# Sums over the first attention's products: one strided reduction, or halving adds in place

## The reference, cut to what matters

```python
pQ = elu(Q); pK = elu(K)                    # Q, K, V: [b, s, H, HD]
Q1, Q2 = split(pQ, 2, axis=-1)
K1, K2 = split(pK, 2, axis=-1)
kv1 = einsum('bshe,bshd->bsed', K1, V) * SCALE
kv2 = einsum('bshe,bshd->bsed', K2, V) * SCALE
w1 = einsum('bshe,bsed->bshd', Q1, kv1)
w2 = einsum('bshe,bsed->bshd', Q2, kv2)
attn = w1 - lmb * w2
```

## Time and profile before

| what | us |
|---|---|
| median of the two runs | 4460.06 |
| span of the profiled execution | 4458.2 |
| DVE busy over the span | 2525.6 (57%) |
| POOL busy over the span | 1256.7 (28%) |
| PE busy over the span | 3281.8 (74%) |
| L818, sum of 13 heads, 56 times | 324.6 |
| L815, sum of 3 heads, 56 times | 81.1 |
| L207 on DVE, product of 13 heads, 56 times | 253.8 |

### The profile page before, as it was taken

How to read it: one execution, slowest core, us unless ns; L and a number is a source line. 1 busy time by engine, 2 the same in 40 slices (tenths; PEclk the granted TensorE clock), 3 DMA queues, 4 the chain that set the end, 5 groups by cost and what they waited for, 6 DMA issues and landing times. The chain is left out here.

```text
span 4458.2 us, 53612 instructions
## 1 busy us (share of the span) xinstructions
PE 3281.8 (74%) x17032; PEld 1909.6 (43%) x17033; DVE 2525.6 (57%) x4655; ACT 1616.7 (36%) x3717; POOL 1256.7 (28%) x873
## 2 busy tenths in 40 slices
PE   6667859775977687587759775976774999999910
PEld 5433623452354235333623452453331666666600
DVE  6764857386658656673857486566749111111156
ACT  2435245433634352444236333624440222222222
POOL 6400910271055008201810460064000111111156
PEclk9889979887988798798879887987885999999955
DMA  1130040004000400310040004002212111111156
GB/s 31 21 52 21 1 71 3 21 0 73 2 20 11 63 21 1 48 25 21 1 72 2 20 1 73 2 20 36 28 45 90 47 45 45 45 45 45 43 182 199
DMA packets 172478, 177.41 MB, mean 40 GB/s; under 512 B 31952, under 2 KB 159696, under 8 KB 172240
## 3 DMA queue, kind: packets, MB, share of 16 engines
q1 hardware_dynamic: 159568, 139.78, 14.6%
q0 software_dynamic: 12672, 34.62, 2.6%
HBM read 106.32 MB, written 67.24 MB: 39 GB/s over the span
## 5 line engine op out<-in xcount | busy, mean ns | idle before, releaser
L434 POOL TENSOR_TENSOR work<-QK,VS 128x2048 f32<-128x2048 f32 x128 | 520.1, 4086 | 1734.7 <-DVE QK L764 1734.2
L925 DVE TENSOR_REDUCE NM<-MX 128x1 f32<-128x128 f32 (+7 forms) x1024 | 735.3, 753 | 448.8 <-PE MX L1162 438.5
L652 ACT ACTIVATE PR<-SP_ 128x512 f32<-128x512 f32 (+3 forms) x1536 | 694.0, 489 | 459.8 <-PE SP_ L1196 312.9
L1160 PE MATMUL MX<-KST,work 96*128 96x512 bf16 (+3 forms) x1536 | 444.8, 354 | 270.9 <-DMA work<-scratch_qd 211.5
L1193 PE MATMUL SP_<-work,KST 99*128 99x512 bf16 (+3 forms) x1536 | 469.6, 333 | 69.6 <-ACT PR L652 32.3
L1554 DVE TENSOR_TENSOR AG<-UB,SL 128x512 f32<-128x512 f32 x136 | 94.1, 692 | 500.3 <-PE UB L1584 500.3
L1160 PEld LDWEIGHTS MX<-KST,work 96*128 96x128 bf16 x1536 | 127.3, 103 | 534.8 <-DVE NM L925 225.5
L1209 PE MATMUL OA<-PR,V 128*32 128x512 f32 (+3 forms) x3072 | 327.3, 498 | 3.3 <-ACT PR L652 3.3
L818 DVE TENSOR_REDUCE AT<-work 128x208 f32<-128x3328 f32 x56 | 324.6, 5797 | 0.0
L1070 PE MATMUL OB<-work,ident 128*128 128x256 f32 x1024 | 258.9, 416 | 74.9 <-POOL work L434 74.9
L1531 ACT ACTIVATE SL<-GB 128x512 f32<-128x512 f32 x136 | 81.3, 598 | 602.6 <-PE GB L1584 602.6
(11 more groups left out here) (242 smaller groups left out, 5252.7 us busy)
## 6 DMA issues: line engine op xcount, KB each, us to landing
work<-scratch_qd SPq DMA_DIRECT2D x96, 256.0 KB, 9.4
scratch_y<-Y SPq DMA_DIRECT2D x136, 128.0 KB, 1.7
scratch_qd<-work SPq DMA_DIRECT2D x48, 256.0 KB, 7.7
X<-in_L_attn_x SPq DMA_DIRECT2D x8, 1024.0 KB, 5.7
scratch_x<-X SPq DMA_DIRECT2D x8, 1024.0 KB, 16.2
scratch_h<-A SPq DMA_DIRECT2D x8, 1024.0 KB, 4.6
scratch_flat<-AT SPq DMA_DIRECT2D x8, 1024.0 KB, 6.2
XH<-scratch_x SPq DMA_DIRECT2D x16, 512.0 KB, 4.3
```

The costliest lines, as they stand in the source:

```text
L434: sg["prod1"].by(pool.tensor_tensor(P1[t % 2][:, i * hh * D:(i + 1) * hh * D].rearrange("p (h e d) -> p h e d", h=hh, e=HD), QK[:, t % 3, ...
L652: sg["exp"].by(act.activation(PR[:, n % 8, q0:512], SP_[:, n % 2, q0:512], ACT.Exp))
L925: sg["mx"].by(dve.tensor_reduce(NM[:, qt, h:h + 1], src, AX.X, ALU.max, negate=True))
L1160: m = pe.matmul(out, lhsT, KST[0:MROW, g, k0:k1], start=True, stop=not last)
```

## The change: what it does

Each of the three sums over e becomes four `tensor_tensor` adds, which work in the buffer of the products. Rows 8 to 15 of every head are added onto rows 0 to 7; then 4 rows onto 4; then 2 onto 2; and the last add, 1 onto 1, writes into `AT`. After each of the first three DVE waits for it to be done (signal `fold`), since the next one reads what it wrote. The signals to the other engines are as before and hang on the last add. For 13 heads the adds have 1664, 832, 416 and 208 elements in each partition, for 3 heads 384, 192, 96 and 48, and for the 4 heads of the last tile 512, 256, 128 and 64.

```diff
+                def fold_rows(x, out, done):
+
+                    rows = x.rearrange("p (h e d) -> p h e d", e=HD, d=HD)
+                    n = HD // 2
+                    while n > 1:
+                        sg["fold"].by(dve.tensor_tensor(rows[:, :, 0:n], rows[:, :, 0:n], rows[:, :, n:2 * n], ALU.add))
+                        sg["fold"].settle(dve)
+                        n //= 2
+                    done.by(dve.tensor_tensor(out.rearrange("p (h d) -> p h d", d=HD), rows[:, :, 0], rows[:, :, 1], ALU.add))
+
                 def attended_last():
...
-                    sg["attn"].by(dve.tensor_reduce(AT[:, u, 0:n * HD].rearrange("p (h d) -> p h d", d=HD),
-                                                    P2[:, 0:n * D].rearrange("p (h e d) -> p h d e", e=HD, d=HD),
-                                                    AX.X, ALU.add))
+                    fold_rows(P2[:, 0:n * D], AT[:, u, 0:n * HD], sg["attn"])
...
                     dve.wait_ge(sg["share2"].sem, u + 1)
                     c0 = (H - POOL_HEADS) * HD
-                    sg["attn"].by(dve.tensor_reduce(AT[:, u, c0:D].rearrange("p (h d) -> p h d", d=HD),
-                                                    PP[:, u % 2].rearrange("p (h e d) -> p h d e", e=HD, d=HD), AX.X, ALU.add))
+                    fold_rows(PP[:, u % 2], AT[:, u, c0:D], sg["attn"])
                     sg["prod2"].settle(dve)
-                    sg["attn"].by(dve.tensor_reduce(AT[:, u, 0:c0].rearrange("p (h d) -> p h d", d=HD),
-                                                    P2[:, 0:(H - POOL_HEADS) * D].rearrange("p (h e d) -> p h d e", e=HD, d=HD),
-                                                    AX.X, ALU.add))
+                    fold_rows(P2[:, 0:(H - POOL_HEADS) * D], AT[:, u, 0:c0], sg["attn"])
```

## The result

The changed kernel takes 4747.8 us (median of two, 4747.0 to 4748.6) against 4460.06: a ratio of 1.065, 95% interval 1.063 to 1.067. That is 288 us slower. The forecast was 4752, with a range of 4682 to 4830. The profiled execution has a span of 4746.7 us, beside the 4458.2 of the earlier trace rows.

A forecast was written before the change was run, and what follows sets the result against it. The prediction took a port shared by DVE's two-SBUF-input instructions and POOL as the bound, 12.79 us a step. Lengthened steps add 36.5 us a batch, x 8 = 292, giving 4750 profiled, 4752 us as a median; range 4682 to 4830.

The forecast's parts named there:

- the port: Something two-SBUF-input DVE instructions and POOL instructions both read through, held for the whole instruction; 12.79 us a step before.
- The exclusion: A DVE instruction with two SBUF inputs and a POOL one cannot run together; a 3328-element product holds POOL off 3.49 us.
- The turns: In each step DVE's product and small adds alternate with POOL's instructions, big adds follow undisturbed; a step becomes 18.2 us.
- The price alone: Adds on DVE without POOL: 3.89 us for 13 heads, 1.39 for 3, against 7.15 for both reductions.
- The sum: Losses of steps 2 to 8 and the last tile added up: 36.5 us a batch, x 8 = 292.
- Rival 1: Adds do not collide with POOL: 4400 us to no change, 5%; a gain over 2%, 1%.
- Rival 2: The port is never idle, POOL's work drifting under DVE's other work: 16.95 us a step, 4682 us; 8%.
- rival 3: PE late at a lower clock, sums behind step 7 13 us: 4796; or handovers cost 45 us more; both 4841; 16%.

The follow-up runs named there:

- experiment 3: Kernel before, its reductions kept, with the sums operand turned so that they read neighbours: 4467.7 us, ratio 1.001.
- experiment 1: Changed kernel with one sum made a reduction again: 4826.4 us with only the 3-head sum folded, 4679.2 us with only the 13-head sum.
- experiment 2: POOL's first-attention products replaced by zero fillings, kernels with adds and with reductions: L434 alone 4416.3 and 4404.4 us; all of them 4305.5 and 4401.6 us.

## Why the prediction was right, point by point

- **The bound.** That the port and not DVE sets a step of the kernel before is shown by experiment 3: 2.7 us less work for DVE a step (5.80 to 3.61 and 1.45 to 0.95), no change in time. By the busy shares alone the forecast would have had the wrong sign.
- **The exclusion.** Shown three times: by POOL's fillings, by the operand in PSUM, and by the big adds taking 3.9 and 4.2 us when they stand where the small ones had stood.
- **The turns.** The step was worked out as 18.2 us and is 18.15; the first of POOL's pair as 7.0 and is 6.97 (108.99, next step); the gain fell to 0.73 us in these steps, 1.01 as a mean over all, where "under 1" was said; POOL's wait for `QK` was put at 4.5 us and is 4.97. L434's mean was put at 5.1 us and is 5.02. The adds of 384 and 192 were put at about 4 us and have means of 3.7 and 3.4; that of 1664 was put at 1.9 and has 1.88.
- **The price alone.** 1.39 and 3.89 us were the terms for the adds without POOL; they are 1.40 and 3.89 in the kernel without POOL's reads (93.56 - 89.67). The plain rate for short rows was right.
- **The sum.** Steps 2 to 8 of the first batch were to grow by 36.6 us; they grew by 123.04 - 86.83 = 36.2 (54.50 to 177.54, against 55.42 to 142.25). The closeness is in part luck: step 2 grew by 6.1 instead of 5.9, and step 7 by 5.1 instead of 5.5. Behind these steps the forecast had next to nothing change. The windows of the first batch say that the stretch to the small network's first sum took 19.3 us instead of 21.0, and the next to the rotation 25.1 instead of 27.4, while the second attention and the rest took 3 us more; the batch comes to +35.1. Of the 1.7 us in the first stretch, 1.1 are four adds of the norms (L778), a term that the prediction did not have: they took 2.52 us beside POOL's gains and take 1.43 now, as those are done before. In the second stretch PE's granted clock was 1.00 instead of 0.87, and four groups of its products (before: L1106, 174.17 to 180.90) took 4.3 us instead of 7.3. The cause of the 3 us stays open. That these parts nearly cancel was not foreseen.
- **Rivals.** Rival 1, that the adds do not collide, falls with the small adds of 3.7 us. Rival 2, a port never idle, asked for a step of 17; POOL's wait of 4.97 us in each step is what it overlooked. Of rival 3 one half happened without effect: PE's granted clock over 51 us went from 0.90 to 0.80 (91 to 142 us), but PE's sums behind step 7 did not come late: POOL's last products could start 6.8 us after its share began (156.15 to 162.98), where 7.3 had been reckoned and 13 feared. They began with DVE's product of step 8, at 162.89.
- **What was too narrow.** The place of the last tile's products decides whether they meet the adds. It came out right here and wrong in two expectations: that of the small sum alone in experiment 1 (18 us), and that of the first pair of fillings in experiment 2 (3.5 us a batch, 28 in all).

## What to carry to other kernels

When DVE and POOL work side by side, count for each instruction of DVE how many inputs it reads from SBUF, and look whether durations of equal instructions differ: 3.61 and 4.90 us for one shape were the first clue. Replacing a slow one-input instruction by cheaper two-input ones can cost more than it saves: a step here grew by 5.6 us (12.5 to 18.15, the mean of steps 3 to 6), where the adds alone would have saved 1.9. Each short one can wait for a long one of POOL, so the number of turns and their place matter more than elements. Better remedies here did not raise the count of SBUF inputs: an operand in PSUM, which lowers it, and an order in which the reduction reads neighbours. The second paid only once the first was there.

## What the runs showed of the hardware that was not expected

- Two edits that were worth 0 and 1% apart were worth 3.5% together, for each removed only one of two bounds that lay close together: the port's 12.8 us a step and DVE's 11.5.
- A reduction over the same 3328 elements takes 5.80 us with a step of 16 elements and 3.61 with neighbours; a POOL product of 768 elements takes 1.50 us with one order of its operands' broadcasts and 1.80 with the other.
- With the operand in PSUM, DVE's product of 3328 elements took 3.61 us, no longer than from SBUF.
